# Expert tiles of a routed feed-forward layer: one PSUM bank for each kind of result in place of two in turn

## The reference

```python
x = x + attention(layernorm(x))      # 16 heads of 64, causal, scores clamped by 50*tanh(s/50)
x = x + ffn(layernorm(x))

def ffn(t):                          # t: 8192 tokens x 256
    shared = gelu(t @ sw1 + sb1) @ sw2 + sb2
    probs = softmax(t @ gate_w + gate_b)               # 8 experts
    topk_p, topk_i = top_k(probs, 2)
    combine = zeros(T, 8).at[arange(T)[:, None], topk_i].set(topk_p)
    h = gelu(einsum('td,edf->etf', t, w1) + b1)        # 256 -> 256 per expert
    y = einsum('etf,efd->etd', h, w2) + b2
    return einsum('te,etd->td', combine, y) + shared
```

## Time and profile before

| | |
|---|---|
| runs | 2083.72 us median, 2082.68 to 2085.25 |
| the profiled execution | 2080.42 us |
| its span | 2078.6 us |
| mean granted TensorE clock | 0.98 of full speed |
| TensorE busy | 1922.9 us (93%) |
| VectorE, ScalarE, GpSimd busy | 1527.5, 1415.6, 1030.0 us |
| expert stage | from 1764.3 us to the end of the span |

### The profile page before, as it was taken

How to read it: one execution, slowest core, us unless ns; L and a number is a source line. 1 busy time by engine, 2 the same in 40 slices (tenths; PEclk the granted TensorE clock), 3 DMA queues, 4 the chain that set the end, 5 groups by cost and what they waited for, 6 DMA issues and landing times.

```text
span 2078.6 us, 39943 instructions
## 1 busy us (share of the span) xinstructions
PE 1922.9 (93%) x14653; PEld 1517.5 (73%) x14653; DVE 1527.5 (73%) x2803; ACT 1415.6 (68%) x2170; POOL 1030.0 (50%) x1195
## 2 busy tenths in 40 slices
PE   6799999999999999999999999999999873999998
PEld 4576767676767676767676767676767652999998
DVE  5576878787878787878787878787876885565565
ACT  6677777777777777777777777777777731544444
POOL 3344454545454545454545454545454643444444
PEclk9999999999999999999999999999999995999999
DMA  4000010101010101010101010101010124764664
GB/s 132 1 11 11 11 42 11 42 11 42 11 42 11 42 11 42 11 42 12 41 13 40 14 39 15 38 16 37 16 37 6 37 72 134 232 189 132 196 183 140
DMA packets 73665, 112.51 MB, mean 54 GB/s; under 512 B 9715, under 2 KB 52218, under 8 KB 73476
## 3 DMA queue, kind: packets, MB, share of 16 engines
q1 hardware_dynamic: 58468, 67.86, 11.3%
q0 software_dynamic: 15008, 42.10, 5.4%
HBM read 63.10 MB, written 48.65 MB: 54 GB/s over the span
## 4 chain that ended last, share of the span: by engine, by line
PE 81%; ACT 12%; DVE 5%; issue 2%; DMA 1%; POOL 0%; SPq 0%; POOLq 0%; DVEq 0%
PE bank_o L1239 12%; PE ring L1218 7%; PE ring L1145 6%; PE ring L1151 6%; PE ring L1146 6%; PE ring L1197 6%; PE ring L1223 6%; ACT prob L585 3%; PE acc L1262 3%; PE ring L1204 3%; PE acc L1264 3%; PE acc L1270 3%; ACT prob L591 2%; PE bank_d L1253 2%; PE ring L1404 2%; PE ring L1409 2%
## 5 line engine op out<-in xcount | busy, mean ns | idle before, releaser
L508 POOL TENSOR_SCALAR_AFFINE_SELECT prob<-prob 128x256 f32<-128x256 f32 x512 | 231.1, 473 | 567.7 <-ACT prob L591 567.6
L585 ACT ACTIVATE prob<-ring 128x1024 f32<-128x1024 f32 (+1 forms) x384 | 326.3, 875 | 205.5 <-PE ring L1223 202.3
L591 ACT ACTIVATE prob<-prob 128x1024 f32<-128x1024 f32 (+1 forms) x384 | 342.7, 915 | 5.2
L520 POOL TENSOR_TENSOR key_sum<-prob 128x768 f32<-128x768 f32 x128 | 243.0, 1898 | 205.6 <-PE bank_d L1253 193.9
L1239 PE MATMUL bank_o<-prob,v 128*32 128x512 f32 (+3 forms) x4096 | 306.6, 440 | 25.1 <-DVE weighed L801 14.4
L1218 PE MATMUL ring<-qT,kT 128*128 128x256 f32 (+3 forms) x1024 | 240.2, 336 | 64.7 <-ACT qT L608 20.0
L780 DVE TENSOR_TENSOR kT<-ring,kT 64x512 fp32r<-64x512 f32 x256 | 176.3, 689 | 153.6 <-ACT kT L598 146.8
L1218 PEld LDWEIGHTS ring<-qT,kT 128*128 128x128 f32 x1024 | 166.6, 191 | 146.5 <-issue 71.2
L1239 PEld LDWEIGHTS bank_o<-prob,v 128*32 128x32 f32 x4096 | 118.0, 110 | 185.1 <-issue 159.1
L796 DVE RECIPROCAL norm<-bank_d 128x512 f32<-128x512 f32 x64 | 214.9, 3357 | 21.7 <-PE bank_d L1253 20.1
L1223 PE MATMUL ring<-q_lo,kT 128*128 128x256 f32 (+3 forms) x1024 | 229.6, 326 | 0.9 <-DVE q_lo L785 0.9
(11 more groups left out here) (224 smaller groups left out, 4689.7 us busy)
## 6 DMA issues: line engine op xcount, KB each, us to landing
xin<-first SPq DMA_DIRECT2D x71, 257.0 KB, 3.1
xin<-second SPq DMA_DIRECT2D x71, 129.0 KB, 2.3
xin<-base SPq DMA_DIRECT2D x71, 128.0 KB, 2.5
x_next<-in_x SPq DMA_DIRECT2D x16, 512.0 KB, 4.6
x_res<-in_x SPq DMA_DIRECT2D x16, 512.0 KB, 4.0
raw_e<-in_w SPq DMA_DIRECT2D x4, 1024.0 KB, 6.7
first<-pad SPq DMA_DIRECT2D x9, 257.0 KB, 4.4
second<-pad SPq DMA_DIRECT2D x9, 129.0 KB, 7.5
```

Of the source, the lines that this page charges most:

```text
L508: last = nc.gpsimd.affine_select(out=diag, in_=diag, compare_op=ALU.is_ge, fill=0.0, base=0, pattern=[[0, 2], [1, P]], channel_multiplier=-1)
L520: nc.gpsimd.tensor_tensor(sums[:, :, :], t0[:, :, P:N], t13[:, :, 0:N - P], ALU.add).then_inc(sum_steps, 1)
L585: nc.scalar.activation(probs[p % PROBS][u][:, :, :], slot[:, :, 0:UNIT_COLS[u]], ACT.Tanh, scale=SCALE / SOFTCLAMP).then_inc(act_emptied, 1)
L591: nc.scalar.activation(cols, cols, ACT.Exp, scale=SOFTCLAMP).then_inc(exp_done, 1)
```

## The change

Each kind of result gets one bank: `bank_o` for transposed inputs, `acc[:, 0]` for hidden products, `bank_d` for transposed hidden rows, `acc[:, 1]` for output products. The two tiles of `ring` are no longer used in this stage. TensorE waits for the readers of the tile before, from n = 1 on.

```diff
 in_high / in_low:
-                bank = (bank_o, bank_d)[n % 2]
-                               bank[:, 0:D].rearrange("p (c t) -> p c t", c=DC)
+                               bank_o[:, 0:D].rearrange("p (c t) -> p c t", c=DC)
 activate:
-                nc.scalar.activation(act_out[n % 2][:, :], ring[0][:, n % 2, 0:FF], ACT.Gelu).then_inc(h_done, 1)
+                nc.scalar.activation(act_out[n % 2][:, :], acc[:, 0, 0:FF], ACT.Gelu).then_inc(h_done, 1)
 act_high / act_low:
-                               ring[1][:, n % 2, 0:FF].rearrange("p (c t) -> p c t", c=FC)
+                               bank_d[:, 0:FF].rearrange("p (c t) -> p c t", c=FC)
 weigh:
-                nc.vector.scalar_tensor_tensor(y_out[n % YOUT][:, :], acc[:, n % 2, 0:D],
+                nc.vector.scalar_tensor_tensor(y_out[n % YOUT][:, :], acc[:, 1, 0:D],
 turn_in:
-                if n >= 2:
-                    pe.wait_ge(in_lo, n - 1)
-                bank = (bank_o, bank_d)[n % 2]
+                if n >= 1:
+                    pe.wait_ge(in_lo, n)
                 for c in range(DC):
-                    last = pe.transpose(bank[:, c * P:(c + 1) * P], ...
+                    last = pe.transpose(bank_o[:, c * P:(c + 1) * P], ...
 expert_hidden:
-                if n >= 2:
-                    pe.wait_ge(h_done, n - 1)
-                expert_product(ring[0][:, n % 2, 0:FF], xinT[n % 2], w_e1, 0, weights_at_tile[n],
+                if n >= 1:
+                    pe.wait_ge(h_done, n)
+                expert_product(acc[:, 0, 0:FF], xinT[n % 2], w_e1, 0, weights_at_tile[n],
 turn_hidden:
-                if n >= 2:
-                    pe.wait_ge(act_lo, n - 1)
+                if n >= 1:
+                    pe.wait_ge(act_lo, n)
                 for c in range(FC):
-                    last = pe.transpose(ring[1][:, n % 2, c * P:(c + 1) * P], ...
+                    last = pe.transpose(bank_d[:, c * P:(c + 1) * P], ...
 expert_out:
-                if n >= 2:
-                    pe.wait_ge(y_ready, n - 1)
-                expert_product(acc[:, n % 2, 0:D], actT[n % 2], w_e2, 1, weights_at_tile[n],
+                if n >= 1:
+                    pe.wait_ge(y_ready, n)
+                expert_product(acc[:, 1, 0:D], actT[n % 2], w_e2, 1, weights_at_tile[n],
```

More of the change, by code:

```diff
@@ L688, in in_high @@
                     act.wait_ge(h_full, n - 1)
-                bank = (bank_o, bank_d)[n % 2]
                 nc.scalar.copy(xinT[n % 2][0][:, :, :],
-                               bank[:, 0:D].rearrange("p (c t) -> p c t", c=DC)).then_inc(in_hi, 1)
+                               bank_o[:, 0:D].rearrange("p (c t) -> p c t", c=DC)).then_inc(in_hi, 1)
             def activate(n):
@@ L703, in act_high @@
                 nc.scalar.copy(actT[n % 2][0][:, :, :],
-                               ring[1][:, n % 2, 0:FF].rearrange("p (c t) -> p c t", c=FC)).then_inc(act_hi, 1)
+                               bank_d[:, 0:FF].rearrange("p (c t) -> p c t", c=FC)).then_inc(act_hi, 1)
             count = len(TILE)
@@ L1105, in in_low @@
                 dve.wait_ge(in_hi, n + 1)
-                bank = (bank_o, bank_d)[n % 2]
-                nc.vector.tensor_tensor(xinT[n % 2][1][:, :, :], bank[:, 0:D].rearrange("p (c t) -> p c t", c=DC),
+                nc.vector.tensor_tensor(xinT[n % 2][1][:, :, :], bank_o[:, 0:D].rearrange("p (c t) -> p c t", c=DC),
                                         xinT[n % 2][0][:, :, :].bitcast(F32), ALU.subtract).then_inc(in_lo, 1)
@@ L1112, in act_low @@
                 nc.vector.tensor_tensor(actT[n % 2][1][:, :, :],
-                                        ring[1][:, n % 2, 0:FF].rearrange("p (c t) -> p c t", c=FC),
+                                        bank_d[:, 0:FF].rearrange("p (c t) -> p c t", c=FC),
                                         actT[n % 2][0][:, :, :].bitcast(F32), ALU.subtract).then_inc(act_lo, 1)
@@ L1393, in turn_in @@
                 pe.wait_ge(xin_loaded[n % XIN], 16 * (n // XIN + 1))
-                if n >= 2:
-                    pe.wait_ge(in_lo, n - 1)
-                bank = (bank_o, bank_d)[n % 2]
+                if n >= 1:
+                    pe.wait_ge(in_lo, n)
                 for c in range(DC):
-                    last = pe.transpose(bank[:, c * P:(c + 1) * P], xin[n % XIN][:, TOKEN + c * P:TOKEN + (c + 1) * P],
+                    last = pe.transpose(bank_o[:, c * P:(c + 1) * P], xin[n % XIN][:, TOKEN + c * P:TOKEN + (c + 1) * P],
                                         ident[:, :])
@@ L1434, in turn_hidden @@
                 pe.wait_ge(h_done, n + 1)
-                if n >= 2:
-                    pe.wait_ge(act_lo, n - 1)
+                if n >= 1:
+                    pe.wait_ge(act_lo, n)
                 for c in range(FC):
-                    last = pe.transpose(ring[1][:, n % 2, c * P:(c + 1) * P], act_out[n % 2][:, c * P:(c + 1) * P],
+                    last = pe.transpose(bank_d[:, c * P:(c + 1) * P], act_out[n % 2][:, c * P:(c + 1) * P],
                                         ident[:, :])
```

## The result

The changed kernel takes 2088.16 us (median of 10 runs, 2086.35 to 2092.78) against 2082.73 for the kernel before (10 runs, 2078.63 to 2085.25): ratio 1.003, 95% interval 1.002 to 1.004. That is 5.4 us slower; 5.2 were forecast.

What follows compares the result with a forecast made beforehand. TensorE's own instructions were taken to set the pace. Register loads 1.7, start 1.7 and end 1.8 sum to 5.2 us, on the median of 2083.72 giving 2088.9 us, range 2085.5 to 2096.

Steps and rivals of the forecast that it cites:

- part 2: Middle of the expert stage: all four nearer waits are over before TensorE arrives, so they cost nothing.
- The 0.25 us to spare: Steady tile: the closest wait, for weigh before the next output product, has slack 0.48 against a hand-over of 0.23 us.
- the Trainium skill's rule: Independent matmul groups should rotate through different PSUM banks; taken kind by kind it would mean a loss in every tile.
- part 3: Every eighth tile: register loads held back make the hidden product 0.10 us late, 17 times, 1.7 us (0 to 4.3).
- the transpose's wait holds it until 1900.46: Before a register load: the input transpose's wait for in_low holds the sequencer, leaving 0.96 us until the hidden product.
- part 4: Start of the stage: uncovered waits for in_low and the first two GELUs cost 1.7 us (0.6 to 2.2).
- from the fourth on ... the slack holds: Start of the stage: from the fourth hidden product, output products lie between and the steady tile's slack returns.
- The clock rival: Start of the stage: new gaps hold the clock at 1.2 GHz longer, losing up to 2 us more, 2091; chance 8%.
- part 5: End of the stage: waits for act_low and weigh make the last output product 1.8 us late (1.6 to 2.1).
- and with it the last weighing and store: End of the stage: the last weighing and store come late by the last output product's 1.8 us.
- part 6: Stop between the two passes, 6.50 us waiting for a DMA: all four kinds are free when it ends, cost nothing.
- The low end of the range: 2085.5 us: 3.5 us if register loads cost nothing, or 2.2 with all low bounds, less run spread of about 1.

Runs made afterwards that it cites:

- outputs alone: The kernel before with only the output products in one bank, their wait one tile nearer; stage 314.0 us against 307.4 in its first profile.
- the four of the table: Single bank for only inputs, hidden products or output products in the kernel before (stages 311.6, 309.6, 314.0 us); register load ahead of input transpose in the changed kernel (316.1).
- hidden products alone: The kernel before with only the hidden products in one bank, their wait one tile nearer; stage 309.6 us against 307.4 in its first profile.

## Why the prediction was right, point by point

**The steady tile (part 2).** Right. Ordinary tiles stay at 2.09 us with all four waits one tile nearer, and the hand-over behind weigh measured 0.20 where 0.23 was taken. The 0.25 us to spare are bounded from both sides: 0.14 us more leaves the ordinary tile as it is, and 0.35 us more brings it from 2.09 to 2.16, which leaves 0.28 to spare. On the Trainium skill's rule (Perfetto Trace Analysis, Optimizing Tensor Performance, Matmuls) the traces say both: four kinds in four banks rotate enough to hide the readers in the ordinary tile of this stage, and with a reader 0.35 us later the second bank of a kind is what hides it.

**Register loads (part 3).** The size was right: 1.8 us in 16 undisturbed intervals (0.11 each; the 15 of the table away from tile 120, and 0.06 at the one just ahead of the stop) against 1.7 in 17 (0.10 each). The cause was told by half. The step "the transpose's wait holds it until 1900.46" names in_low alone; the runs show that the wait for weigh, one product earlier in the sequencer's list, holds it just as long (outputs alone), and that the loss stays when the load is put ahead of in_low's wait. In the tile above weigh ends at 1801.5 and in_low at 1802.1, and the sequencer, held at weigh's wait, would by the spacing of its instructions (0.11 us) have come to in_low's wait at 1802.1 in any case. Both waits happen to put the load at the same place, so the number came out; that was luck.

**The start (part 4).** Forecast 1.7, and mis-sized. In the two first profiles the difference is 2.3 (9.64 less 7.31), against the mean of three profiles of the kernel before (8.18) it is 1.5, but both mix the waits with the turn of the clock. The third hidden product is a better place to look, as the clock is still low there in the second and third profile of the kernel before and in both of the changed one. It stands 6.13 and 6.30 us behind the first transposes before, 7.70 and 7.76 after: 1.5 later, where 1.73 was worked out. The waits and their hand-overs are as worked out too (0.12 behind in_low, 0.24 behind the GELU). But the step "from the fourth on ... the slack holds" took this lateness as kept. The fifth transposes are only 1.0 later (9.65 against 8.62 in these profiles). So at least 0.5 us is made up by then. The clock rival is not settled: the clock came up after 7.8 us in both profiles of the changed kernel, after 4.5, 7.3 and 7.4 in the kernel before. Late turns need no new wait, and whether the waits add to them these profiles can't tell.

**The end (part 5).** Forecast 1.8, measured 1.87 up to the last output product. The step "and with it the last weighing and store" is wrong for the store. From that product to the end of the span the kernel before takes 7.0 us in each of three profiles, the changed one 6.3 in both. In the kernel before the last store waits for GpSimd, which still has the store of tile 140 to do (they start 1.28 us apart), and so begins 0.70 us later behind its weigh than in the changed one (1.50 against 0.80). Of TensorE's lateness 0.7 us falls into this wait, and 1.2 us remain.

**The stop (part 6).** Right for the waits: the same waits for the DMA, and the four intervals around it (two ahead, its own and the next) sum to 16.59 us before and 16.65 after, the 0.06 being a register load. What the part left out is the clock. It came up late behind the stop in two of three profiles of the kernel before, which makes the mean of the kernel before 0.5 us longer there than the changed one.

**What was left out.** The disturbance near tile 120, 0.3 us in one profile and 1.2 in the other.

Together: from the first transposes to the end of the span the kernel before takes 314.4, 316.4 and 316.5 us, the changed one 320.9 and 320.0, 4.7 more by the means. The parts give 1.5 for the start, 1.8 for the loads, 1.9 for the end and 0.8 for the disturbance, less 0.5 behind the stop and 0.7 at the last store: 4.8. The medians differ by 5.4; the rest is what lies before the stage, in code that is alike, where the stage begins anywhere between 1760.9 and 1768.2 us in these profiles. The agreement of 5.2 with 5.4 is thus in part luck: the store's 0.7 is missing from the forecast, part of the start comes from the clock, and the disturbance was not foreseen. The low end of the range, too, does not follow from its own terms: 2.2 less 1 over 2083.72 is 2084.9, not 2085.5.

## What to carry to other kernels

A second buffer that no wait ever needs in the steady tile can still be at work: it is the lead that lets an engine's sequencer do its own slow steps (here a register load of 0.6 us each eighth tile) and that covers a reader's late turn. So count the slack of every wait against the hand-over and against what the waiting sequencer has to do next, and look at the distance of like instructions, since a gap of 0.1 us has no idle time of its own in the profile. Which buffer may be single is decided by place. Single banks for the hidden products and transposed hidden rows cost some 1.95 us together in the timed run, at the start and end. What is left of the 5.4, some 3.5 us, goes with the inputs and outputs, whose waits precede the register load or order the last tiles. This is a difference of two differences, each with an interval of about 2 us to either side, and inputs and outputs together were not run; the timelines carry the reading.

## What the runs showed of the hardware that was not expected

- TensorE's sequencer does not run past a wait that is not met: in the tile above weigh ends at 1801.52 and the wait for it stands at 1801.56, in_low ends at 1802.08 and its wait stands at 1802.12. One wait two steps earlier uncovers a step just as well as the one directly ahead. A register load takes 587 to 827 ns, and its loss is the same 0.11 to 0.12 us per load whether in_low, weigh or both hold it.
- The turn of the clock after a stop of some 17 us of TensorE: 4.5 to 7.4 us after work resumes in three profiles of one kernel, with start stretches from 7.3 to 8.7 us. A difference of 1 us in such a stretch says nothing of the change.
- Near tile 120 the register load takes about 0.8 us in eight of the nine profiles with any nearer wait (648 ns in the ninth) and under 0.6 us in the five with two banks of each kind. Loads of over 0.7 us stand elsewhere as well, such as 815 ns at the fourth load with hidden products alone. The cause was not found.
- In the same place ScalarE begins up to 2 us late in five profiles, with nothing named: the first of the changed kernel and the four of the table that ran on one chip. None of the eight from the other chip has it, the second profile of the changed kernel among them. So it does not belong to the kernel alone; chip and kernel were not tried apart for the others. GpSimd stands still for 3.8 us in that region in every profile, the kernel before included, and what links these is open.
